# Attention and a mixture-of-experts layer on one core: one TensorE signal per chunk of the feed-forward stage, and result scatters tied to a later one

## The reference

```python
x = _layernorm(x + _L0_attn_ref(x, Wq, bq, Wk, bk, Wv, bv, Wo, bo, pos_bias))
# _L0_ffn_ref, E = 8, TOP_K = 2, hidden width 256:
logits = xt @ router_w.T
topk_vals, topk_idx = jax.lax.top_k(logits, TOP_K)
g = jax.nn.sigmoid(topk_vals); g = g / (g.sum(axis=-1, keepdims=True) + 1e-10)
for e in range(E):
    ge = jnp.sum(jnp.where(topk_idx == e, g, 0), axis=-1)
    h = jax.nn.silu(xt @ w_gate[e]) * (xt @ w_up[e])
    out = out + ge[:, None] * (h @ w_down[e])
x = _layernorm(x + out)
```

## Time and profile before

| | us |
|---|---|
| median of 3 runs | 729.98 |
| lowest and highest | 729.13, 731.42 |
| span of the profiled execution | 841.8 |

### The profile page before, as it was taken

The page is one execution under the profiler, slowest core; times in us unless marked ns, Lnnn a source line. Parts: engine busy times, 40 slices in busy tenths (PEclk is TensorE's granted clock), DMA queues, the critical chain, the costliest instruction groups (busy, mean ns, idle before and its releaser), DMA issues.

```text
span 841.8 us, 33526 instructions
## 1 busy us (share of the span) xinstructions
PE 671.6 (80%) x13466; PEld 525.3 (62%) x13466; DVE 504.7 (60%) x1622; ACT 365.0 (43%) x544; POOL 437.6 (52%) x486
## 2 busy tenths in 40 slices
PE   4589999999999989999999978866778787887300
PEld 1356666666667666666666657866677777886300
DVE  6647766777676757786677653655444444544274
ACT  2134434444444434444443334634344445554165
POOL 6522155546545526555654563555555555455465
PEclk9699999999999969999999986989979999989655
DMA  6884454464345434456454030322233222221294
GB/s 167 240 243 117 125 154 123 131 174 133 119 137 137 151 100 131 120 138 188 123 132 125 27 79 30 116 63 72 70 105 90 77 76 78 73 70 58 71 408 152
DMA packets 83576, 103.54 MB, mean 123 GB/s; under 512 B 15488, under 2 KB 70144, under 8 KB 83424
## 3 DMA queue, kind: packets, MB, share of 16 engines
q1 hardware_dynamic: 67008, 70.20, 29.7%
q0 software_dynamic: 8640, 17.84, 6.6%
q10 hardware_dynamic: 7776, 13.37, 4.4%
HBM read 60.12 MB, written 40.79 MB: 120 GB/s over the span
## 4 chain that ended last, share of the span: by engine, by line
PE 54%; issue 14%; DVE 13%; another core or an unknown queue 7%; ACT 4%; POOL 3%; DMA 2%; ACTq 1%; SPq 0%; DVEq 0%; POOLq 0%
PE o_ps L1374 6%; PE score_ps L1316 4%; PE ctx_ps L1388 4%; PE scoret_ps L1334 4%; PE score_ps L1327 4%; PE o_ps L1368 3%; PE bank L1243 3%; PE o_ps L1498 3%; PE bank L1301 3%; DVE neg_max L853 3%; PE scoret_ps L1351 3%; PE scoret_ps L1316 2%; PE ctx_ps L1498 2%; DVE h_sb L1116 2%
## 5 line engine op out<-in xcount | busy, mean ns | idle before, releaser
L304 POOL DMA_INDIRECT slots<-rows_sb,slot_at x128 | 129.8, 1014 | 153.1 <-PE o_ps L1374 96.0
L569 POOL DMA_INDIRECT results<-scaled_sb,result_at x142 | 136.5, 961 | 122.8 <-DVE scaled_sb L1127 86.8
L853 DVE TENSOR_REDUCE neg_max<-score_ps 128x16 f32<-128x1024 f32 x109 | 132.8, 1218 | 90.6 <-PE score_ps L1316 88.5
L729 ACT ACTIVATE prob<-scoret_ps 128x1024 f32<-128x1024 f32 x109 | 111.7, 1025 | 147.8 <-PE scoret_ps L1316 134.4
L1374 PE MATMUL o_ps<-v_sb,prob 128*64 128x18 f32 x2048 | 77.9, 216 | 3.7 <-issue 3.6
L1374 PEld LDWEIGHTS o_ps<-v_sb,prob 128*64 128x64 f32 x2048 | 73.8, 147 | 4.8 <-issue 4.4
L765 ACT CAST w_slot<-wgu_sb 128x1024 fp32r x71 | 74.9, 1056 | 0.3 <-issue 0.3
L1388 PE MATMUL ctx_ps<-diag,o_sb 128*64 128x64 f32 x896 | 57.4, 242 | 16.3 <-DVE o_sb L868 11.6
L1334 PE MATMUL scoret_ps<-bias_hl,fold 128*128 128x512 f16 x218 | 68.6, 398 | 0.0
L1388 PEld LDWEIGHTS ctx_ps<-diag,o_sb 128*64 128x64 f32 x896 | 40.6, 142 | 36.1 <-issue 29.0
L1498 PE MATMUL o_ps<-wd_sb,h_sb 128*128 x288 | 43.5, 299 | 20.7 <-DVE h_sb L1116 18.1
(11 more groups left out here) (188 smaller groups left out, 1599.5 us busy)
## 6 DMA issues: line engine op xcount, KB each, us to landing
stack<-scratch SPq DMA_DIRECT2D x32, 512.0 KB
blocks<-scratch SPq DMA_DIRECT2D x126, 128.0 KB
scratch<-qk_hl SPq DMA_DIRECT2D x92, 128.0 KB
xin<-slots SPq DMA_DIRECT2D x71, 130.0 KB
blocks<-results ACTq DMA_DIRECT2D x16, 512.0 KB, 9.7
scratch<-qk_hl ACTq DMA_DIRECT2D x36, 128.0 KB
x_sb<-in_x SPq DMA_DIRECT2D x16, 256.0 KB
out<-y_sb SPq DMA_DIRECT2D x16, 256.0 KB, 3.4
```

What stands on the lines that cost most here:

```text
L304: nc.gpsimd.indirect_dma_start(slots, bass.IndirectOffsetOnAxis(ap=slot_at[:, k % 2, n:n + 1], axis=0), rows_sb[:, k % 2, n // TT, n % TT, ...
L569: pool.indirect_dma_start(results, bass.IndirectOffsetOnAxis(ap=result_at[s % RBUF][:, t:t + 1], axis=0), scaled_sb[:, s % RBUF, t, :], No ...
L729: act.activation(prob[:, (par + u) % 2, :], turned_scores(i, u)[:, :, :].rearrange("p b c -> p (b c)"), ACT.Exp).then_inc(exp_done, 1)
L853: dve.tensor_reduce(neg_max[:, par, :, v, :], ps[:, :, :].rearrange("p b (h k) -> p b h k", k=W), AX_X, ALU.max, negate=True).then_inc(max ...
```

## The change

TensorE gives one signal for each chunk, `chunk_ps`, on its last instruction of `gate_up(s)` and `turn(s+2)`; the four others go (`xt2_ps` stays for the first two turns). The down product of chunk s-2 stands first in chunk s, where that of s-1 stood last; the two that are left at the end signal `chunk_ps` each. ScalarE and VectorE wait for `chunk_ps` in place of the old four: `silu(s)` and `hidden(s)` for the end of chunk s, `high(s)` for that of chunk s-2, `scale(s)` for that of chunk s+2. GpSimd waits for `scaled` and then for the end of chunk s+3 before the two scatters of chunk s. `deviation` goes ahead of the first scatters.

```diff
-        gate_ps, up_ps, silu_done, h_done = sem("gate_ps"), sem("up_ps"), sem("silu_done"), sem("h_done")
-        y_ps, scaled, result_out = sem("y_ps"), sem("scaled"), [sem(f"result_out{n}") for n in range(RBUF)]
+        chunk_ps, silu_done, h_done = sem("chunk_ps"), sem("silu_done"), sem("h_done")
+        scaled, result_out = sem("scaled"), [sem(f"result_out{n}") for n in range(RBUF)]
@@ results_out
                     pool.wait_ge(scaled, s + 1)
                     settle(pool)
+                    if s + LATE + 2 <= SLOT_CHUNKS + LATE:
+
+                        pool.wait_ge(chunk_ps, s + LATE + 2)
+                        settle(pool)
@@ GpSimd's order
                 for s in range(SLOT_CHUNKS):
-                    results_out(s)
                     if s == 0:
                         deviation(STEPS - 1)
+                    results_out(s)
@@ weights_in, high, silu
-                    after(act, up_ps, s + 1 - WBUF)
+                    after(act, chunk_ps, s + 1 - WBUF)
-                    act.wait_ge(xt2_ps, s + 1)
-                    after(act, up_ps, s + 1 - HBUF)
+                    if s < 2:
+                        act.wait_ge(xt2_ps, s + 1)
+                    else:
+                        act.wait_ge(chunk_ps, s - 1)
-                    act.wait_ge(gate_ps, s + 1)
+                    act.wait_ge(chunk_ps, s + 1)
@@ low, hidden, scale
-                    after(dve, up_ps, s + 1 - HBUF)
-                    dve.wait_ge(up_ps, s + 1)
-
-                    after(dve, y_ps, s + 1 - HBUF)
+                    dve.wait_ge(chunk_ps, s + 1)
-                    dve.wait_ge(y_ps, s + 1)
+                    dve.wait_ge(chunk_ps, s + 3)
@@ TensorE's order
-                e_of = None
+                e_of = []
-                    e_before, e_of = e_of, table_value(pe, expert_at, s, E - 1)
-                    gate_up(s)
+                    e_of.append(table_value(pe, expert_at, s, E - 1))
+
+                    if s >= LATE:
+                        down(s - LATE, e_of[s - LATE])
+                    last = gate_up(s)
+                    if s + 2 < SLOT_CHUNKS:
+                        last = turn(s + 2)
+                    last.then_inc(chunk_ps, 1)
...
-                    if s + 2 < SLOT_CHUNKS:
-                        turn(s + 2)
-                    if s:
-                        down(s - 1, e_before)
-                down(SLOT_CHUNKS - 1, e_of)
+                for s in range(SLOT_CHUNKS - LATE, SLOT_CHUNKS):
+                    down(s, e_of[s]).then_inc(chunk_ps, 1)
```

More of the change, by code:

```diff
@@ L1472, in turn @@
                         last = pe.transpose(turned_ps(s)[:, q * P:(q + 1) * P], xin[:, s % XBUF, q, 0:DM], ident[:, :])
-                    last.then_inc(xt2_ps, 1)
+                    if s < 2:
+                        last.then_inc(xt2_ps, 1)
+                    return last
                 def gate_up(s):
@@ L1480, in gate_up @@
                     b, w = s % HBUF, s % WBUF
-                    for n, signal in ((0, gate_ps), (1, up_ps)):
+                    for n in range(2):
                         for hh in range(2):
@@ L1487, in gate_up @@
                             last = pe.matmul(out_ps, w_slot[:, w, 0, cols], x_hi[:, b, :], start=False, stop=True)
-                        last.then_inc(signal, 1)
+                    return last
                 def down(s, e):
@@ L1499, in down @@
                                              start=(c == 0), stop=(c == 1))
-                    last.then_inc(y_ps, 1)
+                    return last
                 for k in range(2):
```

## The result

| | kernel before | changed kernel |
|---|---|---|
| median of 20 runs, us | 732.36 | 735.42 |
| ratio, 95% interval | | 1.0046 (1.0024 to 1.0069) |
| profiled execution: span, us | 841.8 | 734.4 |

The account below looks back on a forecast made before the run. Feed-forward was taken as bound by TensorE at 2.55 us a chunk, GpSimd close at 2.53, without stalls in the timed run. Other parts cost 0, GpSimd's later start 3: 729.98 + 3 = 733.0 us, range 709 to 739.

Parts of the forecast that it names:

- GpSimd's later start: Feed-forward: GpSimd's new wait delays its scatters, paid at the end; 3 us taken, between 1.8 and 4.3.
- the prediction's step: GpSimd's chunk 5, kernel before: maxima 1.4 us after TensorE's chunk 7, then power and next scatter, 3.4 us in all.
- The shift: GpSimd's scatters, feed-forward: two chunks later less a step, 4.3 us; 1.8 after the power if GpSimd is never idle.
- 0 to 3 in all, and nothing where GpSimd is behind anyway: First 14 feed-forward chunks: VectorE's extra pieces can eat the 0.6 us slack of `low`, at most about 1 us each.
- the slack of the product, the weights and `low`: Feed-forward chunk: slack after the signal of 0.98, 1.2 and 0.6 us, so all hidden, cost 0.
- So most stalls belong to the profiled execution: Feed-forward: of 91 us of stalls in the trace, the timed run has none likeliest, 0 to 16 plausible, 40 at the end.
- The account of times: Timed 729.98 against span 841.8 leaves 626 us for attention and feed-forward, against 738 in the trace.
- Signals dropped: TensorE in feed-forward: dropping 213 signals is worth 0; the skill's 26.3 ns each would give 5.6 us lower.
- For the profiled execution: Traced feed-forward: 3.0 to 3.3 us a chunk, stage 213 to 234 us in place of 272, span 780 to 805.
- In it the rows show release: Argument against held signals costing time: each pair of scatters leaves a pause, in which signals are let through.
- rival 2: Feed-forward: GpSimd's descriptors straight behind every signal hold it, chunk 3.0 us, not 2.55; 746 half-way, 762 at the end; chance 0.08.
- Rival 1: Feed-forward: timed run has stalls too, from runs of four to six scatters; change removes them; 717, 693 to 728; chance 0.34.

Follow-up runs that it names:

- h1: Kernel before with GpSimd's 142 result scatters replaced by powers that write no descriptors, zeros written out instead: 718.39 us.
- h2: Changed kernel with GpSimd's 142 result scatters replaced by powers that write no descriptors, zeros written out instead: 724.77 us.
- a1: Changed kernel, unaltered, beside the kernel before in a series with held signals: 815.27 us, ratio 0.9811.

## Why the prediction was right, and where not

- The sum, +3.0 us, from GpSimd's later start: measured +3.4. That GpSimd sets the end is as forecast; the rows above show it for the changed kernel. No trace of the kernel before in a free series exists, so its side is worked out. In h1, where the power and what leads to it are as before, GpSimd's work of chunk 5 starts at 512.00, 27.1 us behind the first gate product (484.86); the prediction's step, 3.4 us behind TensorE's chunk 7, gives 23.9 + 3.4 = 27.3. Chunk 10 follows 5 x 2.53 later, at 39.8 to 39.9. In the changed kernel it starts at 522.55 - 479.16 = 43.4. The difference is 3.5 us. That is an account that fits, not a measurement of both sides: the first chunk alone takes 4.1 us in h1, 3.5 in the changed kernel and 2.6 in h2, so it can be out by a microsecond.
- What is in it is not what the prediction has in it, and that 3 came near 3.4 is in good part luck. GpSimd's chunk 10 waits for the turn in TensorE's chunk 13. In h1 that turn ends at 524.67, 39.8 us behind the first gate product; with 0.76 to answer, GpSimd would start at 40.6. So the wait itself is worth some 0.7 us here, not 1.8 to 4.3. In the changed kernel the turn ends at 521.79, 42.6 behind: the other 2.8 us are TensorE's lateness, which the wait turns into GpSimd's.
- Two terms were mis-sized, then. The shift was put too high because the prediction takes the down product to stand in a new place: `gate_up(70)` doesn't start 0.81 later, and the signal of chunk s+3 comes one down product (0.81) before the end of the old chunk s+3, which makes 3.5 of the 4.3. And TensorE's loss, "0 to 3 in all, and nothing where GpSimd is behind anyway", was 2.8 us by chunk 13 and counted in full; with GpSimd out of the way it is 6.6 in the whole stage. I had traced the slack of the product, the weights and `low`, and left out the register load ahead of the down product, behind which 2.5 of the changed kernel's 2.9 us by chunk 14 lie (five idle times of 0.20 to 0.64 us).
- "So most stalls belong to the profiled execution" was wrong. The account of times behind it was right, that 730 us have no room for 91 us of stalls; the cause is that the trace and the timed runs came from series of two kinds. The rule of the Trainium skill in "NOTIFIC — the notification-queue block", section 7.1, by which the block holds its producers back rather than lose a record inside, doesn't explain it: the changed kernel is profiled in 736 us with no signal held in feed-forward, at about the same number of recorded instructions (33596, against 33526 in the trace before).
- Signals dropped: worth 0 was said. No run changes only their number. TensorE's chunk is 2.55 us with four signals and with one, so this case shows no price for them. With the 26.3 ns that the Trainium skill gives for a signal ("TensorE: Matmul & The Clock Gate", section "The cost: per-tile semaphore tail") the kernel would have gained an estimated 5.6 us.
- For the profiled execution 3.0 to 3.3 us a chunk, 213 to 234 us for the stage and a span of 780 to 805 were forecast. The free trace has 193 and 734.4. With held signals the later part has 3.23 a chunk as forecast, but the stage is 247 and the span 812.9: against h1 the first 36 chunks lose 34 us and the last 34 lose 22. VectorE's pieces and GpSimd's eight last scatters into `slots` stand in the first part; which of them costs it wasn't separated.
- "In it the rows show release", against rival 2: right. Held signals didn't turn the wait into a loss; with them the change gains 1.9% and the wait alone 2.7 to 2.9%. Rival 1's mechanism is real in these series and absent in the ones that set the result.
- GpSimd ends 14.6 us behind TensorE (672.1 to 686.7); twelve scatters end there and not the four of a GpSimd without a queue.

## What to carry to other kernels

Before a stall in a trace is worth a change, see whether the trace's span and the timed median are of one kind: 842 against 730 said that they weren't. Where an engine has work for 99% of another's time, it can't catch up: whatever makes it late is paid at the end. Before you price a new order, write out the sequence of instructions of both kernels: here the matmuls hadn't moved at all, and what had, a register load of 0.85 us and a few waits, was in no term. And when a trace names the wait ahead of an instruction, see whether what it waits for had come long before.

## What the runs showed of the hardware

GpSimd's indirect DMAs can hold up TensorE's signals, and in some series don't. With held signals, six scatters in a row kept one back for 4.4 us (662.18 to 666.62 in the earlier trace rows) and four for 2.2 (in a1, a turn that ends at 663.20, its silu at 665.35). Release came 0.98 us after the last of four scatters in a1, but in the earlier trace rows the silu starts 0.13 us before the last scatter's end and the product 1.4 us after it, and a second signal in a1 came at the end of the first scatter of a run, so there is no one rule for it here. In a1 ScalarE's and VectorE's signals went through at once meanwhile: with a scatter running, 0.04 us from the end of the silu (667.65) to the product (667.69), and 0.14 from the end of the product (666.72) to the down product (666.86). In the free trace of the changed kernel a signal in feed-forward takes 0.04 us, in the middle of a scatter too. One chip did both, in two series. What sets the kind of a series is open; it wasn't found in the runs here, and no kernel here could choose it.

A register load in TensorE's program takes 0.30 us at the median and 0.94 at most (h2, 71 of them), and 0.85 us pass from the start of one of 0.30 to the matmul behind it (511.14 to 512.00). Between chunks 15 and 28 of h2 TensorE stands nowhere for it (2.55 us a chunk), and ahead of six down products in the first 45 us it stands for 0.4 to 1.1 us.
